# Four-layer gated cross-attention network on one core: the mixture of layer 0 works through a place map and adds its results to x in DRAM, and layer norms take their roots by a power on GpSimd

## The reference, cut to what matters

```python
def _layernorm(x, axis=-1, eps=1e-05):
    m = jnp.mean(x, axis=axis, keepdims=True)
    v = jnp.var(x, axis=axis, keepdims=True)
    return (x - m) / jnp.sqrt(v + eps)

def _L0_ffn_ref(x, Wr, W1, W2):                  # D 256, F 1024, E 8
    t = b * s                                    # 2048
    cap = max(math.ceil(t * CAPACITY_FACTOR / E), 1)   # 256
    probs = jax.nn.softmax(xf @ Wr, axis=-1)
    eidx = jnp.argmax(probs, axis=-1)
    rank = ...                                   # how many earlier tokens chose the same expert
    keep = rank < cap
    xe = xf[dispatch]                            # (E, cap, D)
    h = jnp.maximum(jnp.einsum('ecd,edf->ecf', xe, W1), 0.0)
    ye = jnp.einsum('ecf,efd->ecd', h, W2)
    ye = ye * (pe * valid)[:, :, None]           # probability of the chosen expert
    y = jnp.zeros((t, d)).at[dispatch.reshape(-1)].add(ye.reshape(E * cap, d))

x = x + tanh(g_xattn[0]) * L0_xattn(_layernorm(x), ctx)
x = x + tanh(g_ffn[0]) * _L0_ffn_ref(_layernorm(x), ...)
...                                              # layers 1 to 3; layer 3's attention part
...                                              # starts with a layer norm with gain and shift of its own
```

## Time and profile before

| | |
|---|---|
| median of 3 runs | 2416.69 us |
| profiled execution, its own time | 2412.36 us |
| its span | 2410.8 us |
| TensorE busy | 2003.7 us (83%) |
| VectorE busy | 1345.0 us (56%) |
| ScalarE busy | 938.4 us (39%) |
| GpSimd busy | 497.4 us (21%) |
| mean granted TensorE clock | 0.915 of full speed |

### The profile page before, as it was taken

How to read it: one execution, slowest core, us unless ns; L and a number is a source line. 1 busy time by engine, 2 the same in 40 slices (tenths; PEclk the granted TensorE clock), 3 DMA queues, 4 the chain that set the end, 5 groups by cost and what they waited for, 6 DMA issues and landing times. The chain is left out here.

```text
span 2410.8 us, 35435 instructions
## 1 busy us (share of the span) xinstructions
PE 2003.7 (83%) x12041; PEld 1505.4 (62%) x12105; DVE 1345.0 (56%) x3335; ACT 938.4 (39%) x1866; POOL 497.4 (21%) x1078
## 2 busy tenths in 40 slices
PE   5992893456877486999999989969979789999998
PEld 4671782444444264666666657855558578888897
DVE  4871005624872774888888865867726563223332
ACT  4220221122334244888888862323333242222232
POOL 0223003030112022222222222110250021222222
PEclk9996995658997798999999999989989899999999
DMA  2004441000002049333333313020000144555585
GB/s 91 1 1 147 141 135 47 1 27 15 1 1 31 1 119 243 87 89 88 89 89 89 89 36 95 1 56 11 1 14 1 35 151 157 173 174 164 162 280 176
DMA packets 163857, 199.28 MB, mean 83 GB/s; under 512 B 41446, under 2 KB 132004, under 8 KB 157537
## 3 DMA queue, kind: packets, MB, share of 16 engines
q1 hardware_dynamic: 152912, 181.64, 25.7%
q0 software_dynamic: 10048, 15.34, 2.8%
q10 hardware_dynamic: 720, 0.07, 0.0%
HBM read 162.38 MB, written 36.77 MB: 83 GB/s over the span
## 5 line engine op out<-in xcount | busy, mean ns | idle before, releaser
L2994 DVE TENSOR_REDUCE l3s_mx<-banks 128x1 f32<-128x1024 f32 x256 | 308.4, 1215 | 30.3 <-PE banks L2893 29.6
L1608 PE MATMUL banks<-l3f_xrt,l3f_w 128*128 128x256 f32 (+1 forms) x1536 | 275.5, 340 | 1.5 <-issue 1.5
L1608 PEld LDWEIGHTS banks<-l3f_xrt,l3f_w 128*128 128x128 f32 x1536 | 248.3, 191 | 26.7 <-issue 1.7
L2893 PE MATMUL banks<-l_stack 128*128 128x512 bf16 x960 | 250.1, 383 | 15.3 <-PEq L44 12.5
L1893 DVE TENSOR_SCALAR l3f_sg<-banks 128x256 f32<-128x256 f32 (+1 forms) x192 | 71.9, 375 | 280.4 <-PE banks L1608 280.4
L222 PE MATMUL banks<-ident,xn_tokens 128*128 128x128 f32 x320 | 64.2, 336 | 172.2 <-DVE xn_tokens L211 146.9
L222 PEld LDWEIGHTS banks<-ident,xn_tokens 128*128 128x128 f32 x320 | 45.6, 170 | 195.8 <-DVE xn_tokens L211 125.4
L2985 ACT ACTIVATE x_features<-banks,l3s_mx 128x1024 f32<-128x1024 f32 x128 | 142.4, 1113 | 25.5 <-DVE l3s_mx L2994 24.1
L2893 PEld LDWEIGHTS banks<-l_stack 128*128 128x128 bf16 x1024 | 100.6, 98 | 80.8 <-issue 16.4
L1675 ACT ACTIVATE l3f_sg<-l3f_sg 128x256 f32<-128x256 f32 (+1 forms) x192 | 72.3, 377 | 201.8 <-DVE l3f_sg L1893 201.8
L2985 ACT ACTIVATE xn_tokens<-banks,l3s_mx 128x1024 f32<-128x1024 f32 x128 | 142.4, 1113 | 19.2 <-DVE l3s_mx L2994 19.1
(11 more groups left out here) (570 smaller groups left out, 3799.8 us busy)
## 6 DMA issues: line engine op xcount, KB each, us to landing
l3f_w<-in_L_ffn_gate_up_w_dram SPq DMA_DIRECT2D x24, 2048.0 KB, 8.3
l3f_w<-in_L_ffn_down_w_dram SPq DMA_DIRECT2D x24, 1024.0 KB, 7.3
l0f_w<-in_L_ffn_W_dram SPq DMA_DIRECT2D x16, 1024.0 KB, 5.6
l_stack<-l_q_part SPq DMA_DIRECT2D x64, 256.0 KB, 6.1
l_stack<-l_k_part SPq DMA_DIRECT2D x64, 256.0 KB, 11.7
l_q_part<-l_stack SPq DMA_DIRECT2D x24, 256.0 KB, 3.1
l_k_part<-l_stack SPq DMA_DIRECT2D x24, 256.0 KB, 3.7
l_values<-l3p_vs SPq DMA_DIRECT2D x16, 256.0 KB, 3.7
```

What stands on the lines that cost most here:

```text
L1608: last = nc.tensor.matmul(ps[:, f % 4, h * PAIR:h * PAIR + size(t)], w1_sb[:, p, dc, h * FF + f * P:h * FF + (f + 1) * P], xrt[:, p, dc, 0 ...
L2893: last = nc.tensor.matmul(ps[:, 2 * (v % SCORES) + h, :], stack[p][0][s][:, r, si * P:(si + 1) * P], stack[p][1][s][:, r, h * 512:(h + 1) ...
L2994: nc.vector.tensor_reduce(mx[:, v % RING:v % RING + 1], ps[:, 2 * (v % SCORES):2 * (v % SCORES) + 2, :].rearrange("p a n -> p (a n)"), AX_ ...
```

## The change: what it does

- **Roots.** `newton_root`, `on_vector` and `two_pairs` go. Every layer norm behind a stage measures on VectorE; GpSimd adds EPS and raises to the power -0.5 (two instructions and a drain); VectorE normalises. In l1a and l1f the normalise of a pair comes one loop step after its measure; in the other stages the places of measure and normalise are as the diff shows. GpSimd's bias and row additions in l1f and l3m1, l3m2 are interleaved with the roots.
- **Two norms in one.** l2f's norm is called with `twice=True`: its root is that of v(1 + EPS) + EPS², the root of a norm of a norm. l3p's first norm goes; gain and shift are applied straight to xn, and `x1` is made by that.
- **Mixture of layer 0.** `stage_top1` takes the place of `stage_experts`: x and xn (with each token's shares behind its row) are written to DRAM; each expert has two blocks of 128 places; a place map is made by 16 matmuls; GpSimd gathers 16 blocks into 16 tiles of their own; VectorE applies ReLU in place of ScalarE; ScalarE scales the output by the share that came with the row; GpSimd adds it to x in DRAM, the two DMAs of an expert after those of the last one have landed; at the end SP reads x back in eight loads, and the norm follows pair by pair. The zero fills and the send of results go.

```diff
-def newton_root(eng, drain, var, v, t, y): ...
-def layer_norm(core, ctx, sem, name, on_vector=False, two_pairs=False):
+def layer_norm(core, ctx, sem, name, twice=False):
     def root(pool, j):
         pool.wait_ge(measured, j + 1)
         if j >= 2:
             pool.wait_ge(normalised, j - 1)
-        newton_root(nc.gpsimd, pool.drain, mv[:, j % 2, :, 1], v[:, 0:2], t[:, 0:2], rs[:, j % 2, :]).then_inc(rooted, 1)
+        p = 2 * (j % 2)
+        if j == 0:
+            nc.gpsimd.memset(t[:, :], -0.5)
+        if twice:
+            nc.gpsimd.tensor_scalar(v[:, p:p + 2], mv[:, j % 2, :, 1], 1.0 + EPS, EPS * EPS, ALU.mult, ALU.add)
+        else:
+            nc.gpsimd.tensor_scalar(v[:, p:p + 2], mv[:, j % 2, :, 1], EPS, None, ALU.add)
+        pool.drain()
+        nc.gpsimd.tensor_tensor(rs[:, j % 2, :], v[:, p:p + 2], t[:, 0:2], ALU.pow).then_inc(rooted, 1)
...
# stage_top1, SP
+                for h in range(2):
+                    sp.dma_start(in_tiles(xn_rows)[:, at, 0:D], core["xn"][:, at, :]).then_inc(xn_sent, 16)
+                load_w1(0)
+                sp.wait_ge(shares_made, 1)
+                sp.dma_start(in_tiles(xn_rows)[:, :, D:ROW], shares[:, :, :]).then_inc(xn_sent, 16)
+                load_w2(0)
+                load_w1(1)
+                for h in range(2):
+                    sp.dma_start(in_tiles(x_rows)[:, at, :], core["x"][:, at, :]).then_inc(x_sent, 16)
+                load_w2(1)
+                fetch(sp, following)
+                for t in range(2, E):
+                    sp.wait_ge(hid_ready, FC * (t - 1))
+                    load_w1(t)
+                    sp.wait_ge(out_ready, t - 1)
+                    load_w2(t)
+                sp.wait_ge(x_sent, 32)
+                sp.wait_ge(added, 16 * BLOCKS)
+                for j in range(PAIRS):
+                    sp.dma_start(core["x"][:, 2 * j:2 * j + 2, :], in_tiles(x_rows)[:, 2 * j:2 * j + 2, :]).then_inc(x_in[j], 16)
# GpSimd
+                pool.wait_ge(xn_sent, 48)
+                pool.wait_ge(places_made, 1)
+                for t in range(E):
+                    for u in range(2):
+                        pool.indirect_dma_start(xr[:, t, u, :], None, xn_rows, place[...], ...).then_inc(rows_in[t], 16)
+                pool.wait_ge(x_sent, 32)
+                for t in range(E):
+                    pool.wait_ge(y_stored, t + 1)
+                    if t >= 1:
+                        pool.wait_ge(added, 32 * t)
+                    for u in range(2):
+                        pool.indirect_dma_start(x_rows, place[...], yt[:, t % 2, u, :], None, ...,
+                                                compute_op=ALU.add).then_inc(added, 16)
+                for j in range(PAIRS):
+                    norm_root(pool, j)
# TensorE
+                nc.tensor.matmul(ps[:, 5, 0:P], tri[:, :], every, start=True, stop=False)
+                for n in range(1, TILES):
+                    last = nc.tensor.matmul(ps[:, 5, n * E:P], ones[:, :], every[:, 0:P - n * E], ...)
+                for n in range(TILES):
+                    last = nc.tensor.matmul(ps[:, 6, 0:2 * BLOCKS], low_hot[:, n, :], spot[:, n]...)
# ScalarE
+                    act.wait_ge(out_ready, t + 1)
+                    if t >= 2:
+                        act.wait_ge(added, 32 * (t - 1))
+                    for u in range(2):
+                        last = nc.scalar.activation(yt[:, p, u, :], ps[:, 4 + p, u * D:(u + 1) * D], ACT.Copy,
+                                                    scale=xr[:, t, u, D + t:D + t + 1])
# VectorE, end
+                for j in range(PAIRS + 1):
+                    if j < PAIRS:
+                        dve.wait_ge(x_in[j], 16)
+                        norm_measure(dve, j, tiles_of(core["x"]))
+                    if j >= 1:
+                        norm_normalise(dve, j - 1, tiles_of(core["x"]), tiles_of(core["xn"]))
...
# l3p, VectorE (GpSimd: norm2_root(k + 2) ahead of its four parts of pair k)
+                affine_and_measure(0)
+                affine_and_measure(1)
+                scale_rows(0)
+                scale_rows(1)
                 for k in range(PAIRS):
                     if k + 2 < PAIRS:
-                        both_norms(k + 2)
-                    for m in range(2 * BANKS):
+                        affine_and_measure(k + 2)
+                    remainder(k, 0)
+                    if k + 2 < PAIRS:
+                        scale_rows(k + 2)
+                    for m in range(1, 2 * BANKS):
                         remainder(k, m)
```

More of the change, by code:

```diff
@@ L695, in layout_l0 @@
     return layout
-def first(t):
-    return isinstance(t, int) and t == 0
-def later(t):
-    return not (isinstance(t, int) and t < 2)
 def copy_bank(nc, dst, bank_ap):
@@ L827, in size_of @@
[L827 to L848 removed]
+        out_ready, y_stored, added = sem("out_ready"), sem("y_stored"), sem("added")
@@ new lines, in stage_top1 @@
+        hots, shares = sb("hots", [P, TILES, E], BF16), sb("shares", [P, TILES, E])
+        top, expert, total, best = sb("top", [P, TILES]), sb("expert", [P, TILES]), sb("total", [P, TILES]), sb("best", [P, TILES])
+        rank, upper, beyond, block_of = sb("rank", [P, TILES]), sb("upper", [P, TILES]), sb("beyond", [P, TILES]), sb("block_of", [P, TILES])
+        first_block = sb("first_block", [P, TILES])
+        hit, spot = sb("hit", [P, TILES, BLOCKS], BF16), sb("spot", [P, TILES, 2, BLOCKS], BF16)
@@ L992, in turn @@
-                def turn(jj, p, size):
-                    t = 2 * jj + p
-                    pe.wait_ge(rows_in[p], 16 * jj + 16)
-                    if not first(t):
+                every = hots[:, :, :].rearrange("p t e -> p (t e)")
+                nc.tensor.matmul(ps[:, 5, 0:P], tri[:, :], every, start=True, stop=False)
+                for n in range(1, TILES):
+                    last = nc.tensor.matmul(ps[:, 5, n * E:P], ones[:, :], every[:, 0:P - n * E],
+                                            start=False, stop=(n == TILES - 1))
@@ new lines, in _ @@
+                dve.drain()
+                tt(block_of[:, :], first_block[:, :], upper[:, :], ALU.add)
+                stt(rank[:, :], upper[:, :], float(-P), rank[:, :], ALU.mult, ALU.add)
+                dve.drain()
+                tt(block_of[:, :], block_of[:, :], beyond[:, :], ALU.add)
+                dve.drain()
+                tt(hit[:, :, :], iota_hi[:, :].unsqueeze(1).to_broadcast([P, TILES, BLOCKS]), over_blocks(block_of[:, :]),
+                   ALU.is_equal).then_inc(found, 1)
@@ new lines, in _ @@
+                dve.drain()
+                tt(spot[:, :, 0, :], hit[:, :, :], over_blocks(first_token[:, :]), ALU.mult)
+                for n in range(0, TILES, TILES // 2):
+                    tt(low_hot[:, n:n + TILES // 2, :], iota_lo[:, :].unsqueeze(1).to_broadcast([P, TILES // 2, P]),
+                       rank[:, n:n + TILES // 2].unsqueeze(2).to_broadcast([P, TILES // 2, P]), ALU.is_equal).then_inc(spread, 1)
+                dve.wait_ge(mapped, 1)
+                ts(place_f[:, :], ps[:, 6, BLOCKS:2 * BLOCKS], float(NONE), None, ALU.add)
```

727 lines of the change are left out of this document (209 added, 518 removed).

## The result

The changed kernel takes 2293.24 us (median of 4 runs, 2290.41 to 2294.41) against 2415.53 us before in the same session (4 runs, 2411.15 to 2417.02): ratio 0.9495, 95% interval 0.9478 to 0.9511. The forecast was 2287 with a range of 2259 to 2320. The profiled execution has a span of 2292.7 us.

The account below looks back on a forecast made before the run. Stages start when all engines finish, so stage savings add; TensorE's largest wait was for VectorE's normalise (146.9 us). Terms summed to 130 us: 2412.4 to 2282, forecast 2287 because the profiled run lay 4.3 below the median; range 2259 to 2320.

Parts of the forecast that it names:

- The new root: Layer norms' add, drain and power on GpSimd: 1.0 us from aggregate to normalise, bounds 0.7 to 4.8.
- l0a, l2a, l3a: Stages with the root already on GpSimd: shorter VectorE stalls before the normalise save 27.5 us together.
- l0f: Mixture of layer 0: head and tail together save 30 us, the expert loop nothing.
- Head: Start of l0f: place map and gathers bring the first turn to 227.8 instead of 245.72, saving 18 us.
- Tail: End of l0f, from TensorE's end to the stage's end: 34.4 instead of 46.5 us, saving 12.
- Loop: Expert loop of l0f: same 512 matmuls, length unchanged at 117 us, nothing saved.
- l1a: Stage l1a: without the root a pair takes 5.6 instead of 7.29 us, saving 12 us, bounds 5 to 15.
- rival 1: Middle stages give back: l3p saves 17, l1a 5 (lower clock), l1f 10; 2306 us, chance 0.15.
- l1f, l2f, l3p, l3m1, l3m2: Later stages, with roots off VectorE and l3p's first norm gone, save 12.5, 4.5, 27, 10 and 6.5 us.
- Rival 2: The power is slow: each us of root above 1.0 costs 24 us; at 4.8 us, 2470; chance 0.04.
- Rival 3: VectorE's port lock holds GpSimd's roots, some 0.5 us for 20 pairs: 2297 us, chance 0.13.
- Rival 4: l0f's gathers wait for the shares behind 3 MB: head saves 8, not 18; 2297 us, chance 0.08.

Follow-up runs that it names:

- experiment 8: Changed kernel with l0f's gathers issued for two experts first, the rest between scatter-adds, instead of all 16 in one run: 2290.61 us, ratio 0.9493.
- experiment 10: Changed kernel with a memset, drain and power on a spare tile right behind l0f's last scatter-add: 2286.19 us, ratio 0.9479.
- experiment 11: Changed kernel plus l1a's later normalise and three unread products, l0f's spread gathers and early first power: 2263.26 us, ratio 0.9379.
- experiment 12: Kernel of experiment 11 with x, w2(1) and the next stage's weights sent once the first expert's rows are turned: 2263.24 us, ratio 0.9364.

## Why the prediction was right, and where it was wrong

The sum was 130 us, the spans show 118.1; eleven of twelve stages came out within 3 us of their term. l1a alone is off by 13.4 us, more than the whole miss of 12; the others missed by up to 3 us in both directions and cancelled, which is in part luck. The forecast of the time was off by less, 6.2 us, because the medians differ by 122.3 us. The range's two ends don't come out of the terms either: their bounds add up to 71.5 us (with nothing for the first term) and 150, not to 94 and 153. By the prediction's own steps:

- **The new root.** Taken as 1.0 us, it is 1.20, and the power 0.71. The value lay at the low end of bounds of 0.7 and 4.8 because the nearest rows were short instructions; that was the right way to choose. Each us above 1.0 was priced at 24 us, and doubling the power gives 27 to 30 us for one us. But these roots lie in part in other places than counted: VectorE waits for two each in l0a, l2a and l3a, not for eight in all, and for all eight in l1a, where the prediction had none.
- **l0a, l2a, l3a.** 27.5 forecast, 27.0 measured (6.2 + 11.1 + 9.7).
- **l0f.** 30 forecast, 27.0 measured, by three terms, of which the head was too high, the tail too low and the loop's was missing; that their sum is off by only 3 us is luck. Head 18: the first turn comes 31.3 us after the start of the stage instead of 48.0, 16.7. Tail 12: 30.9 instead of 46.5 us, 15.6, because the scatter-add lands sooner than the 7 us taken (SyncE goes on 3.2 us after the last issue begins) and the pairs follow each other in 1.6 us instead of 2.05; it would have been 18 without the late first power. Loop "unchanged at 117 us": 121.7. This step was wrong, by 5.3 us in this profile and by 3.0 to 5.6 in the others with this order. The prediction counted the gathers' own time and their transfers, and nothing for what 21 us of issuing do to TensorE beside them; experiment 8 shows that.
- **l1a.** This is the step that failed: 12 forecast, -1.4 measured. "Adding VectorE's work without the root and TensorE's products behind the softmax gives 5.6 us a pair" took two things for granted. One is that the root is covered once it is on another engine; it is not, since its user is the next instruction (1.20 us a pair, and 0.74 of normalise that could lie in the wait for TensorE). The other is the full clock for the products behind the softmax; at the lower one a pair takes 1.5 us more. The experiments add up: 4.54 us with both mended, 1.9 for the order and 1.5 for the clock make the measured 7.99; the prediction's 5.6 lies between the periods with the order mended (4.54 to 6.05). The prediction saw the second (rival 1, and "its products eat most of that"), and gave it 7 us, too little. With the order mended the term was there: 13.6 us under before, and 18.3 with the clock held.
- **l1f, l2f, l3p, l3m1, l3m2.** 12.5, 4.5, 27, 10, 6.5 forecast; 15.2, 5.8, 30.0, 7.6, 6.5 measured. l3p runs at TensorE's pace, 10.8 us a pair as worked out, until the seventh pair; then DMA binds, as the prediction said it would be next: 7 us ahead of the last pair and 9.2 us at the end of the stage (10.2 before). The stage's mean DMA share of 0.69 hides that.
- **The rivals.** Rival 1 took l1a further than it said (-1.4, not 5); l3p met DMA and still gave 30, not 17. Rival 2 is out (0.71 us). Rival 3 costs 0.07 us where it shows, but for one root. Rival 4 isn't seen: the head is 1.3 us short of its term, and what the gathers wait behind is x, not the shares.

## What to carry to other kernels

Moving an operation to another engine hides it only if its user is not the next instruction of the one that asked for it: write down both engines' orders of work, and count the instructions between the request and the use. Where an engine's pace is set by a chain through TensorE, read the granted clock of that stretch before pricing the products; taking work out of the chain does not raise it by itself. A run of indirect DMAs issued in one go can stop TensorE beside it; here, issuing them in twos, two experts ahead of their use, took the stop away. A mean DMA share of 0.69 did not keep DMA from binding at the end of l3p: read it stretch by stretch.

## What the runs showed of the hardware

- The run of 16 gathers on GpSimd (1.0 us each, 0.3 between) went with a stop of TensorE ahead of the second hidden group, 2.9 to 4.7 us in all eight profiles that had it; where they were issued in twos (four profiles), it waited 0.73 us, as before the change. The mechanism is open.
- The first drain and power on GpSimd after such a run come 2.8 us late, after l1f's ten gathers and its additions 0.98 us, 0.44 or 0.45 once or twice later on (in l2a; in experiment 10's kernel in l3p and l3m1), elsewhere 0.15.
- When TensorE's clock rises in l1f differs between executions of the same l1f code. Two kernels, over 20 us at the same place of the span, first the kernel of experiment 11:

```profile
460.00:480.00 20.00, 19.53 (x82) 15.58 (x83) 6.54 (x17) 4.05 (x10) 8.92 (x15) 0.92 0.00 0
```

then that of experiment 12:

```profile
460.00:480.00 20.00, 19.53 (x52) 14.13 (x53) 2.93 (x7) 2.96 (x7) 4.41 (x8) 0.60 0.00 0
```

TensorE is busy for the same time in both and gets through 82 or 52 products. The stage takes 83.7 or 89.7 us; in nine other kernels of this page it takes 83.5 to 84.0, in two 86.5 and 86.8. The 6 us are of the size by which runs of one such kernel differ (2257.44 to 2265.98 us), and the profiled execution of experiment 12 is one of the long ones; that they are the same 6 us is likely and not shown.
